# Eight dense projections of a graph network: VectorE copies each product out of PSUM one step later

## The reference, cut to what matters

```python
x = x + _L0_gnn_ref(_layernorm(x), edge_index, ...)   # Wq, Wk, Wv, Wskip: 256 -> 1024
x = x + _L0_ffn_ref(_layernorm(x)[None], ...)[0]      # router: 256 -> 8
x = x + _L1_gnn_ref(_layernorm(x), edge_index, ...)   # w0, w1: 256 -> 512
x = x + _L1_ffn_ref(_layernorm(x)[None], ...)[0]      # W_gat and attention: 256 -> 24
x = x + _L2_gnn_ref(_layernorm(x), ...)               # W_self, W_func: 256 -> 514
x = x + _L2_ffn_ref(_layernorm(x)[None], ...)[0]      # router: 256 -> 8
x = x + _L3_gnn_ref(_layernorm(x), edge_index, ...)   # weight, attention: 256 -> 264
x = x + _L3_ffn_ref(_layernorm(x)[None], ...)[0]      # gate: 256 -> 8
```

## Time and profile before

| | |
|---|---|
| median of 3 runs | 9371.92 us (9362.91 to 9375.82) |
| profiled execution, its own time | 9358.96 us |
| its span, first to last instruction | 9357.0 us |
| mean granted clock of TensorE | 0.811 of full speed |
| PE, DVE, ACT, POOL busy | 66%, 66%, 34%, 57% of the span |
| `evacuate` in l0 | 429.9 to 868.4 us |
| in m0 and in l1 | from 2333.1 us; 3100.3 to 3227.5 us |
| in gat and in l2 | 4345.5 to 4436.8 us; 6578.3 to 6726.6 us |
| in m2 and in l3 | 7936.4 to 8099.6 us; 8457.7 to 8583.9 us |
| in m3 | to 8827.3 us |

### The profile page before, as it was taken

How to read it: one execution, slowest core, us unless ns; L and a number is a source line. 1 busy time by engine, 2 the same in 40 slices (tenths; PEclk the granted TensorE clock), 3 DMA queues, 4 the chain that set the end, 5 groups by cost and what they waited for, 6 DMA issues and landing times. The chain is left out here.

```text
span 9357.0 us, 130668 instructions
## 1 busy us (share of the span) xinstructions
PE 6210.0 (66%) x32165; PEld 4643.2 (50%) x32299; DVE 6139.5 (66%) x16852; ACT 3197.5 (34%) x9297; POOL 5314.7 (57%) x5294
## 2 busy tenths in 40 slices
PE   1355777773299656556688888388567776384399
PEld 0122555552278344434466666277445554372387
DVE  8776888887475576665788888511667776635544
ACT  0111888885322200002233333322244444412322
POOL 0361666665655477773777777466377773442522
PEclk9687999996599877776787777599788887596599
DMA  9411666663176333331111111166633334383365
GB/s 299 135 44 61 174 172 171 174 174 103 56 207 202 108 101 101 101 101 50 8 9 10 9 9 9 52 204 183 188 104 103 103 104 99 124 238 104 98 199 165
DMA packets 685777, 1089.77 MB, mean 116 GB/s; under 512 B 139599, under 2 KB 473511, under 8 KB 684892
## 3 DMA queue, kind: packets, MB, share of 16 engines
q0 software_dynamic: 248352, 553.07, 22.5%
q1 hardware_dynamic: 411052, 476.40, 16.5%
q10 hardware_dynamic: 25744, 53.10, 2.0%
HBM read 864.19 MB, written 226.64 MB: 117 GB/s over the span
## 5 line engine op out<-in xcount | busy, mean ns | idle before, releaser
L4064 POOL DMA_INDIRECT gat_edges_rows<-gat_table,gat_room x1080 | 1080.6, 1001 | 329.4 <-issue 323.6
L2715 POOL DMA_INDIRECT l_edges_ring<-pairs,first_room x832 | 841.6, 1011 | 668.2 <-issue 245.1
L1799 POOL DMA_INDIRECT l_sum_rows<-l_feats,l_sum_ix x832 | 827.2, 994 | 335.4 <-issue 227.4
L2226 PE MATMUL l_sum_o<-l_sum_rows,l_sum_s 128*128 128x256 f32 x1664 | 618.9, 534 | 445.3 <-DVE l_sum_s L2269 232.4
L2766 ACT ACTIVATE l_edges_ring<-l_edges_ring,l_edges_weight 128x64 f32<-128x64 f32 x3328 | 816.4, 335 | 0.0
L4231 DVE TENSOR_REDUCE gat_edges_top<-gat_edges_mx 128x4 f32<-128x512 f32 x1080 | 736.0, 686 | 79.6 <-PE gat_edges_mx L4135 76.7
L3867 ACT ACTIVATE m_ffn_ht<-m_ffn_hp,m_ffn_b1t 128x256 f32<-128x256 f32 x800 | 379.4, 475 | 1178.3 <-PE m_ffn_hp L3835 1177.2
L3845 PE MATMUL m_ffn_yp<-m_ffn_w2b,m_ffn_ht 128*128 128x256 f32 x3200 | 739.6, 384 | 43.4 <-ACT m_ffn_ht L3867 42.6
L3835 PE MATMUL m_ffn_hp<-m_ffn_xt,m_ffn_w1b 128*128 128x256 f32 x3200 | 738.9, 384 | 5.8 <-DVE m_ffn_xt L3882 2.9
L2226 PEld LDWEIGHTS l_sum_o<-l_sum_rows,l_sum_s 128*128 128x128 f32 x1664 | 417.8, 265 | 639.7 <-DVE l_sum_s L2269 322.6
L3845 PEld LDWEIGHTS m_ffn_yp<-m_ffn_w2b,m_ffn_ht 128*128 128x128 f32 x3200 | 592.1, 190 | 154.6 <-ACT m_ffn_ht L3867 45.4
(11 more groups left out here) (863 smaller groups left out, 15630.6 us busy)
## 6 DMA issues: line engine op xcount, KB each, us to landing
m_ffn_w1b<-in_L_ffn_W SPq DMA_DIRECT2D x108, 512.0 KB, 4.4
m_ffn_w2b<-in_L_ffn_W SPq DMA_DIRECT2D x108, 512.0 KB
sorted_rows<-count_main_zero ACTq DMA_DIRECT2D x1, 51858.0 KB
m_ffn_xs<-sorted_rows SPq DMA_DIRECT2D x196, 258.0 KB, 3.5
m_ffn_w1b<-in_L_ffn_w SPq DMA_DIRECT2D x32, 1024.0 KB, 6.1
m_ffn_w2b<-in_L_ffn_w SPq DMA_DIRECT2D x32, 1024.0 KB, 5.6
l_proj_taken<-m_by_node SPq DMA_DIRECT2D x42, 768.0 KB, 6.9
m_ffn_b2b<-in_L_ffn_b SPq DMA_DIRECT2D x196, 128.0 KB, 3.3
```

Of the source, the lines that this page charges most:

```text
L1799: pool.indirect_dma_start(rows[:, j, :], None, table, bass.IndirectOffsetOnAxis(ap=ix[:, j:j + 1], axis=0)).then_inc(sem, 16)
L2226: ins = pe.matmul(o[:, j, 0:R], s4[:, slot % G4 if H else slot, j, :], rhs, start=True, stop=True)
L2715: pool.indirect_dma_start(rows(q, 0, 2 * D)[:, j, :], None, table, bass.IndirectOffsetOnAxis(ap=L.src[:, t:t + 1], axis=0)).then_inc(got[q ...
L4064: pool.indirect_dma_start(rows[:, q % RR, j, :], None, table, bass.IndirectOffsetOnAxis(ap=L.src[:, t:t + 1], axis=0)).then_inc(got[q % GS ...
```

## The change

`evacuate` on DVE, `to_sb` on ACT and `store` on SP each have a lag larger by one. PE's stages, `scale`, `copy_t`, `finish_z`, the fronts, the sorter's ticks and the stages of `RouteFollow` keep theirs; the number of buffers stays two. `lead` only says how many steps are written out.

```diff
-        whole = dict(lead=T + late + 3) if front or follow or sorter else {}
+        whole = dict(lead=T + late + 4) if front or follow or sorter else {}
...
-                stages = [(late + 2 * len(z_stores), store)] if stores else []
+                stages = [(late + 1 + 2 * len(z_stores), store)] if stores else []
...
                 if to_sbuf:
-                    stages.append((late + 3, to_sb))
+                    stages.append((late + 4, to_sb))
...
-                stages = [(late, finish_z), (late + 2, evacuate)]
+                stages = [(late, finish_z), (late + 3, evacuate)]
```

## The result

The changed kernel takes 9281.94 us (median of 4 runs, 9278.83 to 9295.43) against 9370.85 us of the kernel before (4 runs). The ratio is 0.9916, with a 95% interval of 0.9903 to 0.9928: 79 us less (67 to 91); the two medians lie 89 us apart, inside this interval. So the runs had to say which of the two it was.

A forecast was written before the change was run, and what follows sets the result against it. It took waits between engines as the bound, with DVE waiting 230 us for PE's products. l0 50, gat and m0, m2, m3 0, l1 6, l2 2, l3 -2 gave 56 us: 9316 us from the median, range 9268 to 9358.

The forecast's parts named there:

- the signs of being wrong that the prediction names: l0's sort waits up over 50 us, l2 or l3 longer by over 10, gat or m0 shorter by over 5.
- The next turn is PE's: l0: transposes and a product stand ahead of the next turn, so 3.7 to 3.9 of 8.7 us is kept, some 42%.
- the 60%: l0: share taken of nine long waits at turns, 62.5 us in sum, between 42 and 65%, giving 37 us.
- the small waits: l0: the other 29 us of waits for PE's product, 45% taken as gain, 13 us.
- more comes back, with PE's clock: Rival: fewer PE gaps leave most l0 products at 3.6 us, PE never late; some 92 us, 9280; chance 0.17.
- gat, m0, m2, m3 at nothing: Waits for PE of 101.4 us end beside waits for ACT's scale; costed at 0, 5 us to either side.
- Up to 101 us if the cover were gone: gat, m0, m2, m3: worth of the hidden waits for PE without the other wait, up to 101 us.
- Forecast 6, 2 and -2 us: Gains in l1 (six chunks), l2 (first chunk) and l3 (stall losses less PE waits): 6, 2 and a loss of 2 us.
- The product that PE was to lose at each border of l2 and l3: During a store stall PE stops one product sooner and DVE meets it again: l2 about cancels, l3 1 us a stall.
- 3 us of PE waits at the start: l3: gain of 3 us set against five long stalls at 1 us, leaving -2.
- 1.0 us a chunk: l1: the 0.60 and 0.41 us waits for PE go, over six chunks, 6 us.
- The slower rival: l1, l2, l3: PE starved by its buffers loses about 4 us at some 18 chunk borders; 9394; chance 0.07.

The follow-up runs named there:

- run 7: Changed kernel with the second half of the contraction left out in l0, 4 matmuls a tile in place of 8; l0 is 403.1 us.
- runs 3 and 4: ACT's scale put ahead of its copy in all eight projections, in the changed kernel (9214.81 us) and in the kernel before (9321.56 us).
- 1: The change in l0 alone, against the kernel before; 9286.6 us, ratio 0.9922.
- 8: Kernel before with the second half of the contraction left out in l0, 4 matmuls a tile in place of 8; l0 is 440.2 us.
- 2: The change in the seven projections other than l0, against the kernel before; 9342.29 us, ratio 0.9983.
- Run 6: Changed kernel with copies, kept copies and stores one more step later in l0, l1, gat, l2, l3, still two PSUM buffers; 9374.24 us, ratio 1.001.
- run 11: Changed kernel with copies, kept copies and stores one more step later in l1, gat, l3 alone, three PSUM buffers there; 11212.03 us on the slower chip.
- kernel 9: Changed kernel with ACT's scale in l0 one step ahead of everything else; 11200.26 us on the slower chip.
- all three edits: Changed kernel, scale before copy in seven projections, four output buffers in l1, l2, l3, scale a step earlier in l0; 11094.56 us (slower chip), elsewhere 9166.83.

## Why the forecast was right, and where it was off

**The mechanism in l0: right.** The copy waits for nothing at a turn, the scale takes over with 2.62 us (2.6 forecast), and the stage's gain is DVE's idle time less that. 91.5 fell to 5.2 (under 25 forecast). The waits ahead of L1747 and L815 were to grow by 20 to 35 us; they grew by 18.4 and -0.9. None of the signs of being wrong that the prediction names showed.

**The size of l0: 50 against 73 us.** The step that failed is "The next turn is PE's", with its 42% kept, mixed with 65% into the 60%. The nine long waits, 62.5 us, left seven waits for the scale of 18.0 us in all (six of 2.62, one of 2.26), which is 71% kept; two of the nine, at the sorter's end, went whole. PE's lateness at the next turn cost next to nothing: L815's wait grew from 2.82 to 3.17 us at the turn that I had worked out and shrank by 0.9 over all of them. Of the small waits I took 45% of 29 us, 13; 29 less the 5.2 left is 24. The two errors are 44.5 - 37 = 7.5 and 24 - 13 = 11 us; 3.6 more came from L815 and L884, which I had not counted. That is 22 of the 23 us. In the pair of turns that I had worked out, PE's sequence was 1.1 us shorter than my sum of its parts (11.5 against 12.6 us): about 0.8 since I had laid the products and the transposes end to end, 0.4 us each, where they overlap (553.77 and 553.99), and 0.3 since the first product took 5.20 us for 5.51. Behind it the sorter's eight transposes took 1.04 where they had taken 1.76. I then laid that pair's loss on others that have more room.

**The clock: the rival's number without its mechanism.** 9280 was the price of "more comes back, with PE's clock". PE's products got 9.1 us shorter in all (216.7 to 207.6), a mean of 681 for 705 ns, far from all at 3.6 us a tile, so even if all 9.1 were on the path they would be an eighth of l0's gain; and run 7, with half of the products and the clock of l0 down to 0.72, keeps l0 at 403. What that rival had right is only that PE is never late at the next turn. With 73 us less for the same matmuls the granted clock reads 0.82 over the stage (396 to 796 us) where it was 0.80 (396 to 870). The Trainium skill has it that small gaps of PE make the clock swing ("TensorE: Matmul & The Clock Gate", section "A second HAM failure mode: psum-queue depth-cycling"); the direction agrees, and it is not what made the gain.

**gat, m0, m2, m3 at nothing: right**, within 0.9 us each. The reason, two waits that cover each other, is shown for gat and m0 by runs 3 and 4. "Up to 101 us if the cover were gone" was far off: with ACT's order changed, the change takes 12.0 us in m0, 7.5 in gat and nothing in m2, which had 3.2 us of it, and in m3, where the wait goes over to the front's loads.

**l1, l2, l3.** Forecast 6, 2 and -2 us. By the mean of the three kernels without the change there (before, 1, 8) and the three with it (change, 2, 7), l1 goes from 147.6 to 138.8, l2 from 170.8 to 165.8 and l3 from 145.3 to 143.2: 8.8, 5.1 and 2.1. The product that PE was to lose at each border of l2 and l3 did come back at `finish_z`, as forecast, with 4.5 and 4.9 us, but cost less than what the step took away; the long waits for stores stayed, as forecast (5.27 us for 5.44, the longest, in l1; 37.4 for 39.1 in l3). The terms that were too small are the gains: in l3 "3 us of PE waits at the start" stood for 6.9 ahead of L1771 in all, near the end of the stage as well, and in l1 "1.0 us a chunk" left out the start and the end of the stage (12.4 in all, less 2.7). For l3 the sign was wrong, by an amount near the spread of the stage.

**The slower rival.** It was right that PE waits for the copies in l1, l2 and l3: by 11.7, 22.5 and 3.3 us more than before. It was wrong in the price: PE had been idle there anyway, ahead of its transposes (60.9, 60.2 and 66.3 us before, 46.7, 38.6 and 58.9 after), and DVE gets 12 us of waits from it over the three stages (2.7 + 4.5 + 4.9) where the rival had 4 us at each of 18 borders. In l0 PE's wait for the copies is 0.0. Run 6 shows the mechanism outweighing the gain, with 20 to 25 us in l1 and in l2, just one step further; run 11 that in gat and l3 PSUM's buffers are the reason. "PSUM — Partial Sum Buffer" of the Trainium skill, which asks for prompt eviction, agrees with run 6 (100 us more over five stages for a second step) and not with the change itself.

**The sum.** 73.3 + 9.6 + 4.7 + 2.1 + 1.1 is 90.8 us in the stages, and the rest of the kernel took 12.7 us more in this execution than in the one before, within the 21 us by which it moves anyway. That gives the 77.9 us of the spans, but for rounding.

## What to carry to other kernels

Where an engine waits for a product that is made in the same step, a step of slack took away all of the wait down to the next thing that this engine needs in the step (71% of the long waits in l0, nothing in gat and m0); look that up in the timeline and subtract it, and do not also charge the producer's lateness unless the consumer's later waits can be shown to grow. Slack wants buffers ahead of it: here one step was worth more than it cost with two PSUM buffers, two steps cost 7 to 28 us a stage, and at most 4 with a third buffer in the stages that had one. That k steps need k + 1 buffers fits this, but no other pair was run. When two waits end together, removing either shows little; test the pair in a two-by-two of edits, and measure stages, whose spread is 0.5 to 5.5 us, rather than the kernel, whose spread is 20.

## What the runs showed of the hardware

Half of the matmuls did not take half of the time: with them left out the granted clock in l0 fell from 0.84 to 0.72 (changed kernel; from 0.82 to 0.67 in the one before, a mixture of the levels of 1.2 and 2.4 GHz that leans further to the lower), and the mean matmul went from 705 to 912 ns in the kernel before.

One chip took 11289 us for the kernel that others run in 9356 to 9371. It is not DVE's own speed: in l0 DVE is busy for 319.7 us on both, and gat took 105.0 us there as elsewhere, while l1 took 186.8 for 137.2 and l0 538.9 for 400. In l0 the copies wait, put down to "issue", which is time for which the profile shows no wait (kernel 9, 425 to 950 us, and then one of these waits):

```profile
L1770 DVE TENSOR_TENSOR l_proj_osb<-l_proj_op,l_proj_bias 128x1024 f32<-128x1024 f32 x49 | 59.9, 1223 | 131.3 <-issue 98.2 <-remote 23.8 <-PE l_proj_op L1714 7.6
```

```profile
627.22 1.23 DVE L1770 TENSOR_TENSOR l_proj_osb<-l_proj_op,l_proj_bias 128x1024 f32<-128x1024 f32 x1 [19.34 <-issue]
```

Before the wait that ends at 627.22 PE's last product was over at 612.2 and ACT's last kept copy at 606.6, so what is left of the three things that `evacuate` waits for is the stores of two tiles before. Those were issued near 572.5 us, and no packet of theirs is seen after 575: by elimination it is not the moving of data that is slow, but how late its end is known. Over the stage the packets of SP's queue take 18.4% of 400 us on the one chip and 13.6% of 539 on the other, 73 us of the 16 DMA engines both times, and l3, which moves 117 to 120 GB/s, takes 143.7 us for 144.3. Nearly all of the extra time in l0 is six waits of 15.6 to 23.8 us between 516 and 655 us; POOL issues its indirect transfers up to 661, and behind that there is no such wait. l3 and gat, which are as long on both chips, have no work on POOL. That the two belong together is a guess from the times; no run tests it, and why the chip differs stays open. The order of the kernels held there too (ratio 0.9834 for all three edits, 0.9798 elsewhere).
